# A four-layer cross-attention kernel: PSUM banks divided four and three instead of three and four, and the step table of layer 2 moved

## What is computed

```python
for layer in (0, 1, 3):                       # 16 heads of 8, 1444 keys
    q, k, v = x @ Wq, ctx @ Wk, ctx @ Wv
    scores = einsum('bshd,bkhd->bhsk', q, k) * 8 ** -0.5    # layer 1: masked
    o = einsum('bhsk,bkhd->bshd', softmax(scores), v)
    x = norm(x + o @ Wo)                      # layer 0 without the last norm, layer 3 without Wo
# layer 2: the same on 100 keys, causal, then
a = layernorm(att + x);  x = gelu(a @ W1 + b1) @ W2 + b2 + a
```

## Time and profile before

| | us |
|---|---|
| median of 3 executions (1050.79 to 1053.68) | 1051.69 |
| the profiled execution, its own time | 1052.03 |
| its span | 1050.2 |
| TensorE busy | 947.4 (90%) |
| VectorE busy | 839.8 (80%) |
| ScalarE busy | 717.6 (68%) |
| GpSimd busy | 372.3 (35%) |
| stages 0 to 5, each | 36.7 to 39.0 |
| stages 6 to 11, each | 35.0 to 35.4 |
| stage 12, stage 13 | 41.9, 53.2 |
| stages 14 to 19, each | 50.4 to 52.1 |
| stages 20, 21, 22, 23 | 41.7, 34.5, 29.1, 23.0 |

### The profile page before, as it was taken

One profiled execution on the slowest core, in us unless ns is written; L12 is line 12 of the kernel. 1 busy time (PEld: TensorE's weight loads), 2 busy tenths in 40 slices (PEclk: granted clock), 3 DMA queues, 4 the chain that ended last, 5 costly groups with the idle time before them and its releaser, 6 DMA issues.

```text
span 1050.2 us, 43883 instructions
## 1 busy us (share of the span) xinstructions
PE 947.4 (90%) x18826; PEld 570.9 (54%) x18826; DVE 839.8 (80%) x1804; ACT 717.6 (68%) x1621; POOL 372.3 (35%) x404
## 2 busy tenths in 40 slices
PE   1889999999989999999998979898979898989996
PEld 1346556656656665666564545555645464555552
DVE  7888988889788888889987777777878787869851
ACT  1147777777767777777776676667666676767786
POOL 3835345444323312332543434334343434212100
PEclk9669999999999999999999999999989898999999
DMA  8422313222232233233313121212121211212100
GB/s 225 110 62 72 83 50 88 78 69 60 78 95 69 89 95 104 66 93 96 96 52 86 35 82 38 68 38 69 43 62 44 69 51 61 71 36 66 52 4 6
DMA packets 63641, 73.75 MB, mean 70 GB/s; under 512 B 8130, under 2 KB 59114, under 8 KB 63318
## 3 DMA queue, kind: packets, MB, share of 16 engines
q1 hardware_dynamic: 63446, 70.92, 24.3%
HBM read 50.35 MB, written 18.15 MB: 65 GB/s over the span
## 4 chain that ended last, share of the span: by engine, by line
PE 66%; DVE 20%; ACT 5%; issue 4%; POOL 3%; DMA 1%; SPq 1%; POOLq 0%; ACTq 0%; DVEq 0%
PE ring L608 25%; PE sexp L608 15%; PE acc L778 15%; DVE mx L1246 7%; PE ring L651 6%; DVE mneg L1252 3%; DVE mx L1244 3%; POOL kbd L517 2%; ACT probs L1030 2%; PE ring L835 1%; PE ring L628 1%; DVE kp L1223 1%; PE ring L789 1%; DMA rows<-in_rows 1%; PE ring L734 1%
## 5 line engine op out<-in xcount | busy, mean ns | idle before, releaser
L1246 DVE TENSOR_TENSOR mx<-ring,mx 120x400 f16<-120x400 f32 (+1 forms) x1056 | 564.8, 566 | 114.6 <-PE ring L608 111.7
L1030 ACT ACTIVATE probs<-sexp 120x400 f32<-120x400 f32 (+1 forms) x1152 | 529.9, 509 | 139.2 <-PE sexp L608 134.6
L608 PE MATMUL ring<-qx,krep 96*32 96x400 f16 (+2 forms) x4608 | 418.2, 348 | 30.7 <-DVE mx L1246 8.1
L608 PE MATMUL sexp<-qx,krep 97*32 97x400 f16 (+2 forms) x4608 | 410.9, 340 | 8.4 <-ACT probs L1030 4.2
L778 PE MATMUL acc<-probs,vx 120*18 120x200 f32 (+1 forms) x4608 | 254.6, 336 | 1.0 <-ACT probs L1030 0.7
L608 PEld LDWEIGHTS ring<-qx,krep 96*32 96x32 f16 (+2 forms) x4608 | 133.8, 98 | 130.4 <-DVE mx L1246 42.7
L608 PEld LDWEIGHTS sexp<-qx,krep 97*32 97x32 f16 (+2 forms) x4608 | 133.4, 97 | 94.3 <-ACT probs L1030 28.4
L778 PEld LDWEIGHTS acc<-probs,vx 120*18 120x18 f32 (+1 forms) x4608 | 133.3, 99 | 65.9 <-issue 5.4
L534 POOL TENSOR_TENSOR qx<-qs,headmask 96x400 f16<-96x400 f16 x96 | 78.8, 849 | 150.0 <-DVE qs L1233 150.0
L497 POOL CAST ct<-ctf 128x480 f16<-128x480 f32 (+1 forms) x69 | 40.4, 585 | 135.1 <-PE ring L651 75.0
L608 PE MATMUL ring<-ct,wk 128*32 128x480 f16 (+1 forms) x864 | 65.4, 389 | 20.7 <-DVE mx L1246 20.0
(11 more groups left out here) (137 smaller groups left out, 865.0 us busy)
## 6 DMA issues: line engine op xcount, KB each, us to landing
krep<-kept SPq DMA_DIRECT2D x144, 120.0 KB, 2.8
ctf<-in_ctxT SPq DMA_DIRECT2D x16, 722.0 KB
kept<-kp SPq DMA_DIRECT2D x48, 240.0 KB, 3.0
krep<-kept SPq DMA_DIRECT2D x72, 121.0 KB, 2.6
kept<-kp SPq DMA_DIRECT2D x24, 242.0 KB, 2.7
nat<-in_ctx SPq DMA_DIRECT2D x8, 720.0 KB
maskexp<-maskmax SPq DMA_DIRECT2D x8, 281.2 KB, 3.4
anymask<-in_mask SPq DMA_DIRECT2D x1, 1128.1 KB, 10.2
```

Source lines behind the costliest of these rows:

```text
L608: last = run(out[g:g + m], w[:, g:g + m], x, **flags)
L1030: act.activation(probs[0:r, j % PR, :], sexp[j % SR][0:r, 0:QW], ACT.Exp).then_inc(sem["probs_ready"], 1)
L1246: op = dve.tensor_tensor(dst, src, dst, ALU.max)
```

## The change

`SR` becomes 4 and `RING` 3. By `VALUES_AT` the values then run at steps 3, 7, 11 and so on. In `AT` the transposed input `xT` goes from step 18 to 13, `q` from 20 to 16, `k1` from 22 to 24, and `v0`, `mk0`, `v1`, `mk1`, `k2`, `mk2` one step later. In `AT2` the scores of layer 2 go from steps 23, 25, 26, 28 to 20, 21, 22, 23, their exponentials and transposes three to six steps earlier, `a` and `o` two steps earlier. In `AT2_FF` `scale` and `at` go one step later, `w2` from 27 to 34, and `h` stays at 19. The sum over the mask is cut into eight pieces of up to 1129 columns in stage 0, at steps 4, 9, ... 39, and the flag is made of their eight sums.

```diff
--- before.py
+++ after.py
@@ -44,7 +44,7 @@
 MASKED = [-30000.0, -1e30]
 VW = 2 * (DH + 1)
 PAIRS = H // 2
-PR, SR, RING = 10, 3, 4
+PR, SR, RING = 10, 4, 3
 PARTS = 96
 
 
@@ -62,12 +62,12 @@
 
 
 NSTEP = NCH * T
-AT = {"ct0": 0, "ct1": 3, "ct2": 6, "O": 7, "k0": 10, "OT": 12, "wo": 15, "xT": 18, "q": 20, "k1": 22, "v0": 24,
-      "mk0": 25, "v1": 27, "mk1": 28, "k2": 30, "mk2": 31, "v2": 33, "power": 25, "scale": 32, "mt0": 36, "mt1": 37, "mn": 41}
-
-AT2 = {"cx": 2, "kqv": 5, "s0": 23, "s1": 25, "s2": 26, "s3": 28, "e0": 29, "e1": 31, "e2": 32, "e3": 34,
-       "pt0": 32, "pt1": 34, "pt2": 35, "pt3": 38, "a": 42, "o": 44, "out": 45}
-AT2_FF = {"out": 0, "scale": 12, "at": 16, "h": 19, "w2": 27}
+AT = {"ct0": 0, "ct1": 3, "ct2": 6, "O": 7, "k0": 10, "OT": 12, "xT": 13, "wo": 15, "q": 16, "k1": 24, "v0": 25,
+      "mk0": 26, "v1": 28, "mk1": 29, "k2": 31, "mk2": 32, "v2": 33, "power": 25, "scale": 32, "mt0": 36, "mt1": 37, "mn": 41}
+
+AT2 = {"cx": 2, "kqv": 5, "s0": 20, "s1": 21, "s2": 22, "s3": 23, "e0": 26, "e1": 27, "e2": 29, "e3": 30,
+       "pt0": 27, "pt1": 29, "pt2": 30, "pt3": 32, "a": 40, "o": 42, "out": 43}
+AT2_FF = {"out": 0, "scale": 13, "at": 17, "h": 19, "w2": 34}
 
 HOLD = {"smax": 1.6, "k": 3.0, "v": 2.0, "ct": 2.0, "O": 2.8, "q": 2.6, "xT": 1.6, "mt": 2.6, "mn": 1.6, "OT": 1.8,
         "wo": 1.8, "mk": 2.0, "cx": 1.8, "kqv": 3.0, "s": 1.8, "pt": 1.8, "a": 1.8, "o": 3.0, "at": 1.8, "h": 6.0, "w": 1.8,
@@ -129,7 +129,8 @@
         warm = sb("warm", [128, 1])
 
         anymask = sb("anymask", [128, B * S * KEYS // 128], U8)
-        maskcount = sb("maskcount", [128, 1])
+        maskcount = sb("maskcount", [128, 8])
+        masksum = sb("masksum", [1, 9])
         maskflag = sb("maskflag", [1, 1], I32)
 
         xall = sb("xall", [S, B, D])
@@ -225,7 +226,7 @@
                           "h2_filled": 1, "h2_read": 4, "w2_filled": 1, "w2_read": 1, "x2_next": 1, "own_2": 7}.items():
             PER[name] = [0, 0, per, 0]
         setup_names = ["ident_in", "wk_in", "x_in", "const_in", "wq_ready", "wv_ready", "pool_ready", "ones_ready", "acc_zero", "wk_ready", "x_ready", "rest_ready", "x_power", "x_root", "setup",
-                       "mask_in_all", "mask_counted", "flag_filled", "flag_ready"]
+                       "mask_in_all", "mask_counted", "flag_filled", "flag_summed", "flag_ready"]
         sem = {name: es.enter_context(nc.semaphore(name)) for name in list(PER) + setup_names}
 
         READ = {"xT": ("xT_ready", 1), "q": ("q_parts", 1), "mn": ("mrow_ready", 1), "O": ("o_read", 1),
@@ -903,9 +904,9 @@
 
             def flag_sum():
 
-                pe.wait_ge(sem["mask_counted"], 1)
+                pe.wait_ge(sem["mask_counted"], 8)
                 ps = begin("flag", None)
-                pe.matmul(ps[0:1, 0:1], maskcount[:, :], ones[:, :], start=True, stop=True
+                pe.matmul(ps[0:1, 0:8], ones[:, :], maskcount[:, :], start=True, stop=True
                           ).then_inc(sem["flag_filled"], 1)
 
             def stage(s, n, masks=False):
@@ -1098,15 +1099,19 @@
                     if s.prep is not None and j == AT["q"]:
                         queries(s.prep)
                     layer2(s, j)
-                    if n == FLAG_STAGE - 1 and j == AT["v2"] + 1:
+                    if n == FLAG_STAGE and j % 5 == 4 and j < 40:
                         act.wait_ge(sem["mask_in_all"], 16)
-                        act.activation(anymask[:, :], anymask[:, :], ACT.Copy, accum_out=maskcount[:, :]
+                        piece = anymask[:, j // 5 * 1129:min(j // 5 * 1129 + 1129, B * S * KEYS // 128)]
+                        act.activation(piece, piece, ACT.Copy, accum_out=maskcount[:, j // 5:j // 5 + 1]
                                        ).then_inc(sem["mask_counted"], 1)
                     if s.top is not None and j == AT["mn"]:
                         maximum_rows(s.top)
                     if n == FLAG_STAGE and j == NSTEP - 1:
                         act.wait_ge(sem["flag_filled"], 1)
-                        act.copy(maskflag[:, :], bank("flag", None)[0:1, 0:1]).then_inc(sem["flag_ready"], 1)
+                        act.activation(masksum[:, 0:8], bank("flag", None)[0:1, 0:8], ACT.Copy, accum_out=masksum[:, 8:9]
+                                       ).then_inc(sem["flag_summed"], 1)
+                        act.wait_ge(sem["flag_summed"], 1)
+                        act.copy(maskflag[:, :], masksum[:, 8:9]).then_inc(sem["flag_ready"], 1)
 
             act.wait_ge(sem["pool_ready"], 1)
             act.activation(warm[:, :], half[:, 0:1], ACT.Exp)
```

## The result

The changed kernel takes 1131.0 us (median of 4 runs, 1120.7 to 1134.9) against 1052.6 for the kernel before: 1.072 times as long, 95% interval 1.068 to 1.077. It is slower, as forecast, but by 78 us and not by 30, and outside the range that was given. The profiled execution has a span of 1133.1 us.

The account below looks back on a forecast made before the run. TensorE was taken to set an ordinary stage, VectorE close behind. The ring, with layer 2's closer steps, costs 66 us and the GELU gives 36; stage sums give +30.5 on 1052.03, so 1082 us, range 1036 to 1108.

Parts of the forecast that it names:

- the first rival: VectorE, not the bank, is behind at most of 114 turns; ring costs 22 us, time 1038; chance 0.20.
- the GELU's 36 us: Around the GELU in stages 13 to 20, TensorE's 2.78 us stall and 1.7 us of low clock vanish: 8 x 4.5.
- the ring's 66 us: All stages but the last: the ring's third bank, with closer layer-2 steps, costs 26 + 16 + 7 x 3.2 + 2.
- the walk: Stage 9 stepped through with new steps and banks: stalls 5.3 us, less 1.6 that vanish, +3.7; without mask copies +2.0.
- `w2`, `a`, `o`: zero: In layer-2 stages these moved steps cost zero, since nothing of the same stage waits for them.
- The same-bank turn costs up to 0.6: A score product reusing the previous score's bank takes 1.0 us where 0.345 is wanted; 114 such turns.
- The normalisation's stall: zero: Layer 2's normalisation, met one step later, gains 0.5 us; three banks give 0.5 back: zero together.
- The mask: zero: Stage 0: eight pieces at 0.25 us cost +2.0, the earlier first exponential gives -1.9: 0.
- The exponentials' bank: Outside the GELU's stages 13 to 20, the fourth exponentials' bank buys next to nothing.
- The clock rival: Every ordinary stage gets a 3.4 us low-clock stretch, 15 x 1.7 = 25 us on top: 1107; chance 0.12.
- The signs: Ordinary stages 37 to 39 us, layer-2 near 50, queries' wait under 20, first exponential 1.9 earlier, no gap over 2 (stages 13-20).
- The row against the rule: Plain stretch's row: three banks suffice, ring costs 0, 1016; skill's rule on rotating banks: the 66 us stand.

Follow-up runs that it names:

- ring_four_again: The kernel after with three banks for the exponentials and four for the ring, values at the steps of after: 1043.4 us.
- banks_only: The kernel before with four exponentials' banks and three ring banks, old step tables and mask sum, but `w2` at step 34: 1132.5 us.
- tables_only: The kernel before with the step tables `AT`, `AT2` and `AT2_FF` of the kernel after, banks and mask sum unchanged: 1043.4 us.
- q_by_stage: As q_s_early, but `xT` and `q` at 13 and 16 only in stages 13 to 20, at 18 and 20 in all others: 1022.8 us.
- q_s_early: The kernel before with `xT` at step 13, `q` at 16 and the four layer-2 scores at steps 20 to 23: 1037.1 us.
- no_turn: The kernel after with a planner rule that a score product never gets the bank of the score product just before it: 1143.6 us.
- scale_later: As q_by_stage, with layer 2's normalisation at step 14 instead of 12 and `at` at 17 instead of 16: 1018.9 us.
- mask_as_before: The kernel after with the mask summed in one instruction before stage 0, as before: 1131.9 us.
- root_first: As q_by_stage, with GpSimd's root for layer 2's normalisation ahead of its spread of layer 2's keys: 1036.1 us.

## Why the prediction was right or wrong

**The direction and its reason** were right: the ring, not the exponentials, sets the time, and the first rival (the ring hardly matters, 1038) fell; it needed under 36 us for the bank, and the bank costs 88 to 91.

**By stages,** in the profiled executions, the kernel after against before:

| | forecast | measured |
|---|---|---|
| stages 0 to 5, 21 and 22 | +16 | +25.3 |
| stages 6 to 12 | +26 | +39.2 |
| stages 13 to 19 | -9 | +19.1 |
| stage 20 | -2.5 | +0.4 |
| until the first exponential, and stage 23 | 0 | +1.9, -3.0 |
| in all | +30.5 | +82.9 |

Both terms of the sum failed. The range let the ring cost a third more than 66 us, 88, and that is about what it costs; the GELU's 36 us had no range, and with 9 in their place the time leaves the range.

**The term that failed first: the ring's 66 us.** It is 91.5 us with three banks of exponentials on both sides, and the kernel after is 88 us above `ring_four_again`. The split shows where:
- Ordinary stages: the walk set new tables and banks against old and had 2.0 us (stages 0 to 5) and 3.7 (6 to 12). Against before they got 3.5 longer (0 to 5) and 5.3 (6 to 11), of which the bank is 3.0 and 4.1 and the moved steps are the rest. The walk's stalls added up to 5.3; what failed is the 1.6 taken off for stalls that vanish, since stage 9 before has 0.77 us of idle time in all. That 5.3 agrees is partly luck: the keys behind `O` wait 0.62 and not 1.2, step 13 waits 0.22, steps 23 (0.48) and 38 (0.44) weren't in the walk, and 1.4 us of the 5.3 is not idle but busy time (34.43 to 35.86). Step 19 (0.98 against 1.1) was right, and steps 29 to 33 were nearly so (1.38 in all against 1.6).
- Layer-2 stages: forecast 3.2, measured 4.5 where the low clock is the same, and 6.0 between the kernel after and `ring_four_again`. What lies between the two is not the ring as such. 34.1 us at half the clock against none is at most 17 us, 2.4 a stage. And VectorE's additions from SBUF (last section) take 7.9 us more in these stages, 1.1 a stage. The two overlap, and how they share the 1.5 isn't shown.
- Until the first exponential: forecast 0, measured +5.9 against `ring_four_again`, with 35.4 us at half the clock against 4.1. That time differs widely between kernels with the same work there (36.9 before, 50.7 in `banks_only`), so how much of it belongs to the bank stays open.

**The term that failed second: the GELU's 36 us.** The steps give 9.
- There was less to gain. The wait for the keys' bank is 2.36 to 2.79 us with 3.4 us of low clock behind it in six of the eight stages; in stages 18 and 19 it is 1.80 and 1.65, with none. That is 19.8 + 6 x 1.7 = 30 us.
- From before to `ring_four_again` stages 13 to 20 gain 24.4 us, 3.1 a stage instead of 4.5. The wait did go, but for stage 20, where TensorE waits 1.95 us for an exponential (0.77 with the exponentials' fourth bank). In stages 13 to 19 TensorE's idle times fell only from 38.9 to 28.3 us: 36 stalls under 1 us stand there instead of 22, and three of 2.3 us that are no GELU's.
- How much of the gain is the clock isn't settled. In that execution up to 20.5 us of it (41.0 us at half the clock before, none with the steps moved); in `tables_only`, with the same steps and four banks, stages 13 to 19 gain 16.1 us and keep 23.9 us of low clock.
- Moving `xT` and `q` in **every** stage had no price of its own in the prediction, only one together with the ring. On four banks (`ring_four_again`) stages 0 to 12 got 14.7 us longer, the mask's pieces in stage 0 among it, and `q_by_stage` measures that move directly: 14.3 us.

So 36 less 6 that weren't there, less 6 that weren't gained, less 14.7 elsewhere is about 9. The reason that the prediction gave the exponentials' fourth bank (TensorE may go on to step 23) isn't needed where the scores of layer 2 stand: `q_s_early` does it with three.

**"`w2`, `a`, `o`: zero."** This failed. At step 34 `w2`'s additions fall between two reductions of the row maxima, and TensorE waits 1.46 us [the timeline at 765.39]; in four of the seven layer-2 stages that stall is followed by 3.4 us at half the clock. The question asked, who of the same stage waits for the step, was the wrong one: what matters is what stands next to it on VectorE. The bank is the smaller part of it. In `ring_four_again` the wait is 0.30 us in stages 14 to 19, where the second addition takes 0.28 us, and 1.11 in stage 13, where it takes 1.09 as in the kernel after.

**"The same-bank turn costs up to 0.6."** The count of 114 times 0.6 agreed with the walk by chance, as was said there; `no_turn` shows that it was no mechanism.

**"The normalisation's stall: zero."** For the kernel after that can't be told apart from its neighbours. What it can be worth is shown elsewhere: `scale_later` gains 3.9 us by moving the step by two.

**The mask: zero.** Right in sum, 1131.9 against 1131.0. The first exponential comes 3 us earlier than in `mask_as_before`, and stage 0 takes 1.4 longer.

**The exponentials' bank: "next to nothing" outside the GELU.** About right: 3.9 us, 3.2 in stage 23, which the prediction didn't name, and 2.7 at the GELU of stage 20, with stages 13 to 19 the other way.

**The clock rival (1107)** was wrong in its place and right in kind. It wanted low clock in ordinary stages; stages 0 to 11 have 15.8 us of it against 13.0 with the fourth bank. The total is that of before, 91.9 us against 90.9, so by the sum the clock explains nothing. By place it does: the 3.4 us stretches behind the GELU are gone, and new ones stand behind the stalls of 1.5 to 2 us.

**The signs.** Stages 0 to 11 went beyond 37 to 39 us (39.3 to 42.9), the layer-2 stages 13 to 19 are at 50.9 to 57.4 and not near 50, the wait of the queries fell to 24.1 and not under 20, and the first exponential comes 1.9 us later and not earlier (78.6 against 76.7). No gap of TensorE over 2 us in stages 13 to 20 came true; the longest is 1.99.

**The row against the rule.** The plain stretch said that three banks are enough, and by that row alone the time would have been 1016. For the stretch itself that holds: after step 38 stage 9 of the kernel after has no stall of 0.2 us. The Trainium skill (Perfetto Trace Analysis, Matmuls and Optimization Strategy) has independent groups rotate through PSUM banks and says that repeated gaps can mean too few buffers. The measurement decides for the rule: 37 gaps under 1 us in six stages, 91.5 us for one bank.

## What to carry to other kernels

A ring of buffers between two engines that are both nearly full must be judged where other products share it, not in its plain stretch: there every further holder takes a bank for the length of its slowest reader, and the stalls are small, many, and move on when one is cured. Before a whole table is changed to repair one kind of stage, change it in that kind alone; here the same two numbers were worth 14 us more that way. And price what a step stands next to on its reader's engine, and beside which work of GpSimd it falls, not only who waits for it.

## What the runs showed that was not expected

**An addition that lasts as long as its neighbour.** VectorE's addition of two arrays in SBUF (`oatt`, `y`, `xall`: 0.28 us alone) lasted 2.52, 2.46 and 2.79 us beside GpSimd's multiplication of 2.86, and 1.10 beside its subtraction of 1.09, and ended within 0.15 us of it each time. In the same stretch the maxima, which read one operand from PSUM, took their 0.57. The trace books it as busy time of VectorE, so it looks like a slow instruction and not like a wait. The Trainium skill (SBUF — State Buffer, Who interferes with whom) says that a VectorE instruction with two SBUF inputs contends with a GpSimd instruction that reads SBUF, and that the one issued second is blocked until the first is done. The trace agrees: GpSimd's instruction had begun first each time, by 0.14 to 0.55 us, and the addition ended with it. The other order stands in `ring_four_again`, stages 14 to 19: the addition `xall` begins 0.01 to 0.02 us ahead of GpSimd's subtraction and keeps its 0.28, and that subtraction takes 1.21 to 1.23 instead of 1.10. So an offset of some 0.15 us changes which of the two is held. In the kernel after 34 such additions last over 0.4 us, and each ends 0.14 to 0.15 us behind an instruction of GpSimd.

`root_first` has 6.9 us more of it in `oatt` (12.3 against 5.4 in eight calls) and 10 us more of low clock in stages 13 to 19, worth up to 5; together that comes near its 13.3 us, worked out from its trace and not tested by itself.

**The clock doesn't follow the length of a stall alone.** The stall of 1.46 us at `w2` is followed by 3.4 us at 0.50 in stages 13, 17, 18 and 19, and by 1.00 in stages 14 to 16. In `ring_four_again` the stalls of 2.28 to 2.37 us at step 14 of stages 17 to 19 are followed by no low clock at all; in `q_by_stage` and `scale_later`, with four banks too, the same three stalls of 2.37 are each followed by 3.4 us of it. A stretch of low clock has to be read from the profile, of more than one execution where it matters; from the gaps it can't be worked out.
